# Feed-forward weights quantised in the latent attention's steps, with query tiles in two PSUM banks and pair weights in one raw buffer

## The reference

```python
x = x + _L0_xattn_ref(_layernorm(x, axis=-1), ctx_512, ctx_512)
x = x + _L0_ffn_ref(_layernorm(x, axis=-1), classifier_w, bias, gate_w, up_w, down_w)
x = x + _L1_xattn_ref(_layernorm(x, axis=-1), ctx_512, Wq, w_kc_q, w_kc_kv, W_qr, W_kr, Wo)
x = x + _L1_ffn_ref(_layernorm(x, axis=-1), w_gate, w_up, w_down)
# latent attention, per head
q_big = _apply_rope(einsum('bshk,hkq->bshq', q_hk, w_kc_q), sin_q, cos_q)
scores = einsum('bhsr,bhlr->bhsl', einsum('bshq,hqr->bhsr', q_big, W_qr), k_r)
ctx_c = einsum('bhsl,bld->bhsd', softmax(scores), kv_r)
# feed-forward; _quantize_mx scales each block of 32 by a power of two from its maximum and rounds the elements
_q_w = lambda w: _quantize_mx(w, 2, 1.0, 2.0, 6.0)
gate, up = _mx_linear(x, w_gate), _mx_linear(x, w_up)      # einsum(_q_act(x), _q_w(w))
return _mx_linear(silu(gate) * up, w_down)
```

## Time and profile before

| what | us |
|---|---|
| median of 3 runs (938.92 to 940.67) | 939.76 |
| profiled execution, whole | 941.17 |
| its span in the trace | 939.6 |
| experts, second to last tanh step (213.83 to 374.35) | 160.5 |
| latent attention, steady part (425.5 to 742) | 316.5 |

### The profile page before, as it was taken

How to read it: one execution, slowest core, us unless ns; L and a number is a source line. 1 busy time by engine, 2 the same in 40 slices (tenths; PEclk the granted TensorE clock), 3 DMA queues, 4 the chain that set the end, 5 groups by cost and what they waited for, 6 DMA issues and landing times. The chain is left out here.

```text
span 939.6 us, 15315 instructions
## 1 busy us (share of the span) xinstructions
PE 818.2 (87%) x4785; PEld 573.2 (61%) x4792; DVE 686.4 (73%) x1250; ACT 397.3 (42%) x1055; POOL 506.4 (54%) x511
## 2 busy tenths in 40 slices
PE   3999999669999999579999999999999888756675
PEld 2454554347767777466777777776777687724443
DVE  5899896569887878756667666666667519999994
ACT  2688887322222222214454444544444542224442
POOL 3555554227565666315555555555555577536664
PEclk9999999779999999869999999999999979979987
DMA  9100000040000000210010101010000000000000
GB/s 267 56 1 0 0 1 1 0 149 18 18 17 17 17 17 0 90 45 30 17 46 1 46 1 46 0 45 0 1 1 1 1 1 1 0 1 17 23 17 33
DMA packets 8751, 24.49 MB, mean 26 GB/s; under 512 B 1711, under 2 KB 4143, under 8 KB 8087
## 3 DMA queue, kind: packets, MB, share of 16 engines
q1 hardware_dynamic: 8154, 23.81, 7.6%
q10 hardware_dynamic: 549, 0.08, 0.1%
HBM read 21.79 MB, written 2.10 MB: 25 GB/s over the span
## 5 line engine op out<-in xcount | busy, mean ns | idle before, releaser
L1122 PE MATMUL ps<-yt_all,a 128*128 128x512 f32 x576 | 140.9, 398 | 0.0
L1284 POOL TENSOR_TENSOR p<-p,l_inverse 128x512 f32<-128x512 f32 x64 | 66.6, 1041 | 125.7 <-DVE l_inverse L1247 125.7
L1122 PEld LDWEIGHTS ps<-yt_all,a 128*128 128x128 f32 x576 | 106.4, 189 | 26.2 <-issue 5.0
L773 PE MATMUL ps<-yt_experts,wsplit 128*128 (+1 forms) x384 | 102.5, 419 | 10.0 <-DVE h L867 8.3
L1202 ACT ACTIVATE p<-ps,l_negmax 128x128 f32<-128x128 f32 x256 | 90.1, 378 | 37.3 <-DVE l_negmax L1254 37.3
L1254 DVE TENSOR_REDUCE l_negmax<-ps 128x4 f32<-128x512 f32 x64 | 41.3, 687 | 81.8 <-PE ps L1165 81.8
L1233 DVE TENSOR_TENSOR turned<-ps,rope 128x1024 f32<-128x1024 f32 x64 | 78.3, 1225 | 29.3 <-PE ps L1122 25.2
L394 DVE TENSOR_REDUCE negmax<-ps 128x4 f32<-128x512 f32 x128 | 85.4, 688 | 11.4 <-PE ps L243 9.6
L773 PEld LDWEIGHTS ps<-yt_experts,wsplit 128*128 128x128 f32 x384 | 75.0, 202 | 28.2 <-DVE inner L861 7.7
L1142 PE MATMUL ps<-q,b 128*128 128x512 f32 x192 | 88.5, 596 | 1.0 <-issue 1.0
L325 ACT ACTIVATE pt<-ps 128x512 f32<-128x512 f32 x128 | 72.8, 597 | 8.2 <-PE ps L263 4.1
(11 more groups left out here) (185 smaller groups left out, 1697.2 us busy)
## 6 DMA issues: line engine op xcount, KB each, us to landing
wide<-in_wide SPq DMA_DIRECT2D x8, 768.0 KB, 4.2
mx_raw<-in_mx SPq DMA_DIRECT2D x8, 384.0 KB, 3.1
x<-in_x SPq DMA_DIRECT2D x4, 512.0 KB, 9.0
ctx_t<-in_ctx_t SPq DMA_DIRECT2D x1, 2048.0 KB, 7.6
narrow<-in_narrow SPq DMA_DIRECT2D x8, 256.0 KB, 4.5
out<-x SPq DMA_DIRECT2D x16, 128.0 KB, 1.7
ktraw<-in_ctx_rows SPq DMA_DIRECT2D x1, 1248.0 KB
wraw<-in_gate SPq DMA_DIRECT2D x1, 1024.0 KB, 18.4
```

The source lines that it names most:

```text
L773: t = pe.matmul(out, w_at(pw, w + k * EXPERTS * INTER + x * INTER, INTER), run_of(m.yt[:, py, k, :, :], j).rearrange("p b s -> p (b s)"), ...
L1122: t = pe.matmul(tile_ps[k], a[par][:, pa, kin, k * 128:(k + 1) * 128], m.yt[:, py, kin, 4 * j:4 * j + 4, :].rearrange("p b s -> p (b s)"), ...
L1284: pool.tensor_tensor(p[:, head, :, :], p[:, head, :, :], spread(inverse[:, head, :], 2, S), ALU.mult).then_inc(normed[head], 1)
```

## The change

1. The quantising of the feed-forward weights leaves `routed_experts` (all of its DVE, POOL, PE, ACT and SP instructions) and is put in the steps of `latent_attention`: a chunk in two steps, powers in even j, rounding in odd j. DVE does it around the inversion of head B.
2. The three query tiles share PSUM banks 0 and 1 (`tile_bank`), so that bank 2 is free for the turned chunk. Tile 2 is multiplied behind the narrowing, and waits until tile 0 has been rotated; tiles 0 and 1 of the next step wait for the rotations of tiles 1 and 2. DVE's three rotations of tile 2 come behind both inversions.
3. `wide` and `narrow` have one buffer each; SP loads those of pair i+1 when pair i's last use of them is over, between the loads of chunks.

```diff
@@ latent_attention, PSUM
+        tile_bank = lambda j, k: m.bank((j + k) % 2)
+        mx_ps, q_ps, s_ps = m.ps[:, 2, :].bitcast(BF16)[:, 0:CHUNK], m.bank(3), [m.bank(4), m.bank(5)]
@@ SP
+            def load_chunk(i, half):
+                wait(sp, mx_made, 2 * i + half - 1)
+                sp.dma_start(raw[half][:, :], d["mx"][i, :, half, :]).then_inc(mx_loaded[half], 16)
+            def load_pair(i):
+                sp.wait_ge(c_made, i)
+                load_wide(sp, m, d, i)
+                sp.wait_ge(b_made, i)
+                load_narrow(sp, m, d, i)
@@ PE, tile and step
-                wait(pe, tile_turned[k], n)
+                if k == TILES - 1:
+                    pe.wait_ge(tile_turned[0], n + 1)
+                else:
+                    wait(pe, tile_turned[k + 1], n)
...
-                    for k in range(TILES):
-                        tile(n, j, par, k)
+                    tile(n, j, par, 0)
+                    tile(n, j, par, 1)
                 extra()
                 if inside(n - 1, STEPS):
...
                     t.then_inc(narrowed, 1)
+                if inside(n, STEPS):
+                    tile(n, j, par, 2)
                 if inside(n - 2, STEPS):
...
+                if j % 2 == 0 and inside(n - 1, STEPS):
+                    turn_chunk(2 * i + j // 2 - 1, 1 - j // 2)
@@ DVE, step
                 invert(n, 0)
                 if inside(n, STEPS):
+                    if j % 2 == 0:
+                        block_powers(i, j)
+                    else:
+                        quantise(i, j, second=False)
+                invert(n, 1)
+                if inside(n, STEPS):
+                    if j % 2 == 1:
+                        quantise(i, j, second=True)
                     dve.wait_ge(tile_made[2], n + 1)
                     wait(dve, q2_made, n)
-                    rotate(4, 2, 4)
-                    rotate(5, 2, 5, slice(CE, 2 * CE), slice(0, CE))
-                invert(n, 1)
-                if inside(n, STEPS):
-                    rotate(5, 2, 5, slice(0, CE), slice(CE, 2 * CE)).then_inc(tile_turned[2], 1)
+                    rotate(4, j, 2, 4)
+                    rotate(5, j, 2, 5, slice(CE, 2 * CE), slice(0, CE))
+                    rotate(5, j, 2, 5, slice(0, CE), slice(CE, 2 * CE)).then_inc(tile_turned[2], 1)
                 extra()
@@ POOL, step, behind the two additions of q01
+                    if j % 2 == 0:
+                        pool.wait_ge(mx_step, MX_STEPS * (2 * i + j // 2) + SCALE_STEPS)
+                        pool.tensor_tensor(chunk, chunk, spread(mx_inverse[:, :], 2, MX), ALU.mult).then_inc(mx_divided, 1)
+                    else:
+                        pool.wait_ge(mx_step, MX_STEPS * (2 * i + j // 2 + 1))
+                        wait(pool, mx_turned, 2 * i + j // 2 - 1)
+                        pool.tensor_tensor(quantised[j // 2][:, :].rearrange("p (n c) -> p n c", c=MX), chunk,
+                                           spread(scale[:, :], 2, MX), ALU.mult).then_inc(mx_made, 1)
```

More of the change, by code:

```diff
@@ L693, in routed_experts @@
         ht = [sb(f"ht{i}", [INTER, 2, N], F32R) for i in range(2)]
[L695 to L698, removed]
         gate_ps, up_ps = [m.bank(0), m.bank(2)], [m.bank(1), m.bank(3)]
         down_ps = m.ps[:, 4:6, :].rearrange("s c (b e) -> s (c b) e", b=2)
-        weight_ps, mx_ps = m.bank(6), m.ps16[:, 1, 0:CHUNK]
+        weight_ps = m.bank(6)
         logit_ps = m.bank(7)[:, 0:B * ROUTES].rearrange("s (b r) -> s b r", b=B)
@@ L739, in _ @@
             sp.dma_start(m.rope[:, :, :], d["rope"]).then_inc(m.rope_loaded, 16)
[L741 to L750, removed]
         @block.tensor
@@ L793, in step @@
                     t.then_inc(down_made, 1)
[L794 to L801, removed]
             for b in range(B):
@@ L1049, in latent_attention @@
         ctx_made, ctx_kept = sem("l_ctx_made"), sem("l_ctx_kept")
+        mx_loaded = [sem(f"mx_loaded{i}") for i in range(2)]
+        mx_step, mx_divided, mx_made, mx_turned, mx_kept = (
+            sem(f"mx_{n}") for n in ("step", "divided", "made", "turned", "kept"))
         block = scope.enter_context(nc.Block())
@@ L1177, in step, with turn_chunk @@
                     t.then_inc(ctx_made, 1)
+                if j % 2 == 0 and inside(n - 1, STEPS):
+                    turn_chunk(2 * i + j // 2 - 1, 1 - j // 2)
+            def turn_chunk(c, buf):
+                pe.wait_ge(mx_made, c + 1)
+                wait(pe, mx_kept, c)
+                for k in range(3):
+                    t = pe.transpose(mx_ps[:, k * 128:(k + 1) * 128], quantised[buf][:, k * 128:(k + 1) * 128],
+                                     m.ident16[:, :])
+                t.then_inc(mx_turned, 1)
             steps(pe, step, prepare)
@@ L1229, in prepare, with mx_then, block_powers @@
                                       ALU.subtract).then_inc(c_lo, 1)
-            def rotate_both(k):
+            def mx_then(instruction, c, k, before):
+                instruction.then_inc(mx_step, 1)
+                dve.wait_ge(mx_step, MX_STEPS * c + before + k)
+            def block_powers(i, j):
+                c = 2 * i + j // 2
+                dve.wait_ge(mx_loaded[j // 2], 16 * i + 16)
+                wait(dve, mx_made, c)
+                then = lambda k, instruction: mx_then(instruction, c, k, 0)
+                w = raw[j // 2][:, :]
+                then(1, dve.tensor_reduce(scale[:, :], w.rearrange("p (n c) -> p n c", c=MX), AX.X, ALU.max,
+                                          apply_absolute_value=True))
+                block_scale(dve, then, scale[:, :], mx_inverse[:, :], 1.0)
```

117 lines of the change are left out of this document (51 added, 66 removed).

## The result

The changed kernel takes 991.96 us (median of 5 runs, 987.54 to 993.33) against 938.92 us (935.41 to 940.67) for the kernel before on the same chip: a ratio of 1.056, 95% interval 1.054 to 1.058. Forecast were 995 us and a range of 968 to 1014. The profiled execution was the fastest of the five: 987.54 us, span 985.7. Against the span of 939.6 before, that is 46.1 us more.

What follows compares the result with a forecast made beforehand. PE was taken to bound the latent attention, while in the experts PE and DVE each waited for the other. The terms: 941.2 - 23 (experts) + 61 (latent stage) + 17 (clock) = 996, 995 by the median; range 968 to 1014.

Steps and rivals of the forecast that it cites:

- Experts, -23: Experts: without quantising PE sets the pace, 21 us off 29 steps and 2 off the stage's end; bounds -20 and -24.
- Tile 2 behind the narrowing: Latent attention: DVE's remainder waits behind tile 2's rotations, so PE stands 2.3 us (j = 2) and 2.45 us (j = 0).
- a sign: Latent profile: PE idle 2.3 to 2.6 us with j 0 and 2, over 3 with j 1; L1229 or L1231 over 1.3.
- Rounding and POOL: Latent odd steps: rounding, with 1.0 us of POOL contention per half, makes PE stand 3.6 us (j = 1), 0.6 (j = 3).
- the upper bound: Latent odd steps: twice the POOL contention, PE standing 5.6 us with j = 1 and 1.6 with j = 3.
- First and last pair: Ends of the latent stage: 3.3 us for the first pair, 1.6 for the last, which prepares nothing.
- The clock, +17: Latent stage: 19 stalls, the clock falling behind 8 of 14 at 1.55 us each, cost 17 us; bounds 0 and 29.
- Rival B: Latent attention: the same stall at full clock, 979 us, 978 by the median; chance 0.19.
- Rival D: Latent attention: the wait for the remainder is free, say because DVE does it ahead of the rotations: 931 us; chance 0.05.
- One buffer, 0: Latent attention's pair weights: one buffer each, loads landing 4.2 us after issue, costs 0; bounds 0 and 2 us.

Runs made afterwards that it cites:

- The experts' side alone: The kernel before without any quantising of the feed-forward weights, wq set to zero once by POOL: 917.76 us, ratio 0.975.
- the filled pauses: The changed kernel with 12 useless identity transposes in each of PE's waits for a remainder: 976.17 us, ratio 1.038 to the kernel before.
- the first experiment: The changed kernel with DVE's remainder of the prepared piece directly behind head B's inversion, ahead of second-half rounding and tile 2's rotations: 931.75 us, ratio 0.992.
- the run with three banks: The changed kernel with a bank per query tile, all tiles at the head of PE's step, DVE's quantising behind the remainder: 936.24 us, ratio 0.997.
- the run with the banks alone: The changed kernel with a bank per query tile and all tiles at the head of PE's step, DVE and POOL order kept: 960.46 us, ratio 1.023.

## Why the prediction was right

**Experts, -23.** Right, and by its reasons. The 29 steps gave 21.5 us of the 21 forecast, 23 of them at 4.79 or 4.80 and the other six between 4.71 and 4.88, no clock under 1.00. From the last tanh to the first transposes of the stage behind, 17.2 us became 15.1, the 2 forecast. The experts' side alone measured 22.6.

**Tile 2 behind the narrowing.** Right in place and size: 2.34 and 2.21 us of pause against 2.45 and 2.3. The full pairs without a fall of the clock took 50.9 us, 8.4 over before; 9.35 was forecast. For six pairs that is 50.5 against 56. 2.21 is a little under the 2.3 to 2.6 that were named as a sign.

**Rounding and POOL.** The term that was too large. At j = 1 PE stood 2.69 us for 3.6, at j = 3 not at all for 0.6. So two of the signs did not come: over 3 us of idle with j = 1, and L1229 or L1231 over 1.3. I had carried over the one contention that the earlier trace rows showed, 1.0 us on a SCALAR_TENSOR_TENSOR. In the latent step it fell on others: L1225 and L1231, both TENSOR_SCALAR, took 1.08 us for 0.36, 0.72 too much each, while L1226 and L1229 beside them ran at 0.56 and 0.53. The second half ended at 8.1 into the step (557.62 - 549.54) where I had 9.0. That is 0.3 behind the 7.8 at which tile 2 is there anyway, so rounding and POOL together cost 0.35 us of stall. The two that were held had started 0.20 and 0.40 us behind POOL's instruction; L1224 and L1229 had started ahead of it, and L1226 between POOL's two. The Trainium skill's "GPSIMD Engine Reference", section "Specifications", has contention for VectorE instructions in a two-port mode or with two SBUF inputs. The trace agrees that a TENSOR_SCALAR can be held up; the upper bound that I derived from it, every one of the five at once, was wrong. The trace of before had shown it too, not for 384 columns but for the 12 of a power (0.17 us elsewhere), beside an instruction of POOL from 227.17 to 229.06, which I had passed over:

```profile
227.58 1.50 DVE L1300 TENSOR_SCALAR mx_scale<-mx_scale 128x12 uint32<-128x12 uint32 x1
```

**First and last pair.** 3.3 and 1.6 were forecast, 6.7 and 6.0 measured. In the first pair I missed a wait: in the second step PE's tile 1 needs the bank that the first step's tile 2 leaves, and these rotations are late behind the powers, two of which (L1317 and L1318, 12 columns) were held up by POOL's additions and took 0.90 and 1.20 us for 0.17:

```profile
396.95 1.66 PE L1074 MATMUL ps<-yt_all,a 128*128 128x512 f32 x6 [2.82 <-DVE turned L1241]
```

I had written of the banks "the next step's tile 1 needs tile 2's (11.1 at worst, needed at 12 or later). Nothing." That is right for a full step. In the first step, without narrowing or transposes, PE gets there 7.5 us into the stage. Without quantising this wait is 0.83 us. The first two steps grew by 2.4 us, the stall of the third and its clock behind it by 4.0, the fourth by 0.3. In the last pair the first three steps grew by 0.39, 0.75 and 0.34, 1.5 in all (from 744.11 to 775.22, 31.11 us, against 29.63 before), where 0.2 and 0.6 had been forecast by turns; 4.5 more lie in the last step and the tail, of which 1.7 are one group of six q matmuls that ran at the lower clock behind a pause of 1.86 us:

```profile
787.76 4.51 PE L1094 MATMUL ps<-q,b 128*128 128x512 f32 x6 [1.86 <-issue]
```

Before, they took 2.81 behind a pause of 1.02. The rest is the fourth step (0.75), that longer pause (0.84), the turning of the last chunk and a longer wait for POOL behind it (1.0), and 0.3 at the end.

**The clock, +17.** Near it for the median, as far as the filled pauses show: they took 15.8 us off, though not every fall in those executions need have stood behind one of the 19. In the profiled execution it fell behind 5 of 19 stalls, as here at 611.25 (the same step took 13.56 us at 549.54 and here 15.82, from 600.40 to 616.22), and cost about 10:

```profile
611.25 1.12 PE L1111 MATMUL ps<-ident,p 128*128 128x128 f32 x4 [2.69 <-DVE a L1194]
612.30 2.08 PE L1119 MATMUL ps<-keys,qs 64*128 64x128 f32 x16
614.31 1.97 PE L1128 MATMUL ps<-l_pt,kvr 128*64 128x128 f32 x16
616.22 3.57 PE L1074 MATMUL ps<-yt_all,a 128*128 128x512 f32 x12
```

Both factors were off, and in opposite senses: fewer falls than 8 in 14, but each in the full pairs cost 2.1 to 2.3 us for 1.55, since four to seven microseconds of matmuls ran at the lower level. (The trace of before has four more pauses of that length than I counted, ahead of 759.58, 806.17, 832.06 and 925.77, the lower level behind three of them.) The mean granted clock of that execution was 0.933, of the four others, 991.35 to 993.33 us long, 0.928 to 0.931: they spent more time at the lower level, though no timeline shows where. Rival B, the same stall at full clock, would be the run with the filled pauses: 976 where it was priced at 978. The rule on pauses for which it stood (the Trainium skill, "TensorE: Matmul & The Clock Gate", section "HAM oscillation — how this bites in real kernels") would have the clock stay up behind all 19; it fell behind 5 of them. Rival D, the remainder ahead of the rotations, is the first experiment: 931.75 where it was priced at 931, with less than its price in the pairs (4.9 for 12 x 0.8) and more at the two ends (9.3).

**One buffer, 0.** Right: ratio 0.999.

**The sum.** Of the profiled execution: experts -23.6 (21.5 and 2.1), six pairs +50.5, clock in them +9.0, first pair +6.7, last +6.0: +48.6, less 1.7 in the stages ahead of the experts' steps and 0.7 in the feed-forward (180.02 to 179.28 us): the span's 46.1, but for roundings. The forecast's errors were -5.5 in the pairs' stalls, +7.8 at the two ends of the stage (1.4 of it one of the five falls, 1.7 the q matmuls above) and -8 on this execution's clock. So the mechanism was right; that 995 came within 3 us of the median is partly luck, for the stall was priced too high, the ends too low, and the errors cancelled.

## What to carry over

Ask of a moved instruction not only whether its own result comes in time, but what stands behind it in its engine's queue: here three rotations stood ahead of a half-microsecond subtraction that the busiest engine needed, and one line's place was worth 60 us. A change that takes work off one stage should be timed in halves (that stage alone, the receiving stage alone); here 22.6 us of gain were hidden under 74 of loss, and 9 to 12 of them came out once the order was mended. Where an engine is busy to the last microsecond, count the first and the last round of its loop apart: the waits that a full round hides are bare there.

## What the runs showed of the hardware

- Beside POOL's normalising (128x512), a TENSOR_SCALAR of 384 f32 columns took 1.08 us where it takes 0.36 alone, and beside POOL's additions (128x512) even 1.34 in the run with three banks, where two SCALAR_TENSOR_TENSOR took 1.57 and 1.51 for 0.56. Which of the five is held up goes with where POOL's instruction falls: L1229 at 0.53 had started 0.16 us ahead of POOL's, L1231 behind it.
- The clock fell behind 5 of 19 pauses of 2.2 to 2.8 us, with quantising and without, behind 3 of 6 of 2.7 to 2.8 in the run with the banks alone, and behind none of the 32 waits for a remainder of 0.5 to 1.4 us in that run and in the filled one. Twice it stood at 0.50 or 0.51 for 6.5 us (454.00 and 611.00) and came back with no further pause.
- Useless matmuls in a pause shortened no step that had run at full clock, kept the clock up in all 19 places, and lowered the median by 15.8 us (the latent stage of the profiled execution by 8.4).
